# Two ScalarE copies in place of four, and two kinds of TensorE work dealt out in turn in a fused deformable convolution

## What is computed

```python
x = x + _L0_conv_ref(_gn(x), ...)
x = x + _L1_conv_ref(_gn(x), ...)

# inside _L1_conv_ref:
value = (xf @ vp_w.T + vp_b).reshape(n, L, G, cg)
om_in = depthwise_conv3x3(x, dw_w) + dw_b
om = om_in @ om_w.T + om_b            # 2*9 offsets and 9 masks for each of 8 groups
sampled = gather(y0i, x0i, (1 - ty) * (1 - tx)) + gather(y0i, x0i + 1, (1 - ty) * tx) \
        + gather(y0i + 1, x0i, ty * (1 - tx)) + gather(y0i + 1, x0i + 1, ty * tx)
out = jnp.einsum('nhwgk,nhwgkc->nhwgc', mask, sampled)
out = out.reshape(n, L, c) @ op_w.T
```

## Time and profile before

| | |
|---|---|
| median of 3 runs | 2926.51 us (2925.91 to 2933.81) |
| the profiled execution's own time | 2924.83 us |
| its span, first to last instruction | 2923.0 us |
| instructions | 100581 |
| PE (TensorE matmul) | 2430.8 us busy (83%), 40456 records |
| PEld (TensorE weight load) | 2021.2 us (69%), 40456 records |
| DVE | 2205.6 us (75%) |
| ACT (ScalarE) | 2259.7 us (77%) |
| POOL | 1917.6 us (66%) |
| mean granted TensorE clock | 0.952 of full speed |

### The profile page before, as it was taken

One profiled execution on the slowest core, in us unless ns is written; L12 is line 12 of the kernel. 1 busy time (PEld: TensorE's weight loads), 2 busy tenths in 40 slices (PEclk: granted clock), 3 DMA queues, 4 the chain that ended last, 5 costly groups with the idle time before them and its releaser, 6 DMA issues. The chain is left out here.

```text
span 2923.0 us, 100581 instructions
## 1 busy us (share of the span) xinstructions
PE 2430.8 (83%) x40456; PEld 2021.2 (69%) x40456; DVE 2205.6 (75%) x3095; ACT 2259.7 (77%) x4721; POOL 1917.6 (66%) x1452
## 2 busy tenths in 40 slices
PE   3999779993688888888888888888888888888887
PEld 2666556772577777777777777777777777777786
DVE  3555423334989897989888898989898988989773
ACT  2444256662989889898989898898989898989892
POOL 1000000003888888888988888888988898988892
PEclk8999889996899999999999999999999999999998
DMA  4555579975577677777777777777778777877675
GB/s 103 130 132 144 143 182 265 263 199 172 124 191 203 181 195 192 188 191 190 204 194 192 187 200 195 197 183 193 199 189 198 188 196 187 206 179 190 177 176 147
DMA packets 356164, 538.18 MB, mean 184 GB/s; under 512 B 171728, under 2 KB 258256, under 8 KB 355536
## 3 DMA queue, kind: packets, MB, share of 16 engines
q1 hardware_dynamic: 296656, 422.71, 60.3%
q10 hardware_dynamic: 59136, 110.11, 10.8%
HBM read 312.82 MB, written 219.77 MB: 182 GB/s over the span
## 5 line engine op out<-in xcount | busy, mean ns | idle before, releaser
L1109 ACT ACTIVATE dwt<-xp,wts 128x224 f32<-128x224 f32 x2016 | 797.3, 484 | 40.8 <-ACT wst L1135 31.8
L1280 PE MATMUL acc_p<-abuf,vbd 128*32 128x136 f32 (+5 forms) x20480 | 710.4, 291 | 54.9 <-issue 46.0
L1280 PEld LDWEIGHTS acc_p<-abuf,vbd 128*32 128x32 f32 (+1 forms) x20480 | 645.9, 145 | 117.7 <-issue 60.5
L979 DVE TENSOR_TENSOR pr<-mh_p,ht 128x864 f32<-128x864 f32 x672 | 668.9, 1051 | 23.2
L1258 PE MATMUL win_p<-pr,smat 128*128 128x160 f32 x4032 | 626.7, 310 | 27.3 <-POOL pr L1065 15.8
L246 PE MATMUL cv<-cin,wb 128*64 128x392 bf16 x6912 | 590.4, 333 | 25.8 <-ACT cin L225 25.8
L1258 PEld LDWEIGHTS win_p<-pr,smat 128*128 128x128 f32 x4032 | 570.4, 194 | 51.2 <-issue 22.4
L246 PEld LDWEIGHTS cv<-cin,wb 128*64 128x64 bf16 x6912 | 401.4, 110 | 208.7 <-ACT cin L225 25.9
L1048 POOL TENSOR_TENSOR dwt<-dwt 128x896 f32<-128x896 f32 x224 | 516.3, 2305 | 4.7 <-ACT dwt L1109 4.7
L1062 POOL TENSOR_TENSOR pr<-pr 128x576 f32<-128x576 f32 x224 | 317.3, 1417 | 187.8 <-DVE pr L979 187.8
L1135 ACT ACTIVATE wst<-win_p 128x200 f32<-128x200 f32 x896 | 388.6, 605 | 62.4 <-PE win_p L1258 38.7
(11 more groups left out here) (132 smaller groups left out, 2674.9 us busy)
## 6 DMA issues: line engine op xcount, KB each, us to landing
abuf<-weight_scratch SPq DMA_DIRECT2D x1568, 96.0 KB, 3.3
weight_scratch<-wst ACTq DMA_DIRECT2D x112, 960.0 KB, 6.2
xt<-x SPq DMA_DIRECT2D x128, 392.0 KB, 7.6
rows_scratch<-vsb SPq DMA_DIRECT2D x224, 128.0 KB, 2.1
vbd<-rows_scratch SPq DMA_DIRECT2D x896, 32.0 KB, 3.2
x_scratch<-xt SPq DMA_DIRECT2D x64, 392.0 KB, 6.6
y<-x SPq DMA_DIRECT2D x64, 392.0 KB, 4.4
x3h<-x_scratch SPq DMA_DIRECT2D x64, 392.0 KB, 4.9
```

The lines of the kernel that those rows point to most:

```text
L979: dve.tensor_tensor(pr[:, j % 2, slots, :, :, :].rearrange("p k e x z -> p e k (x z)"), mh[:, a, :, :].rearrange("p (k x) z -> p k (x z)", ...
L1109: ins = act.activation(dwt[:, j % 2, k, :].rearrange("p (r w) -> p r w", w=W), image[:, r:r + BR, k % 3:k % 3 + W], ACT.Identity, scale=dw ...
L1280: mm = pe.matmul(acc_p[32 * (2 * s + b):32 * (2 * s + b) + 32, 0:2 * TN].rearrange("p (t w r) -> p t w r", t=BR, r=2)[:, t0:t1 + 1, x0:x1, :],
```

## The change

There are four parts, which belong together.

- The order in the last 32 places of the table of offsets and masks becomes (g, k): group, then image row. `copy_om` reads its PSUM source with k innermost, that is with 256 elements between neighbours.
- `win_p` is packed: the five distances follow one another, 800 columns without gaps. The fourth distance (e == 3) then lies across the end of a 512-column bank, so its matmuls are cut into one of 32 and one of 128 columns.
- `copy_weights` takes the 800 columns in two copies of 400 elements, by the parity of the image row, in place of four of 200.
- `apply` and `windows` are dealt out in turn in three parts: four rows of `apply`, then the distances 0 and 1; four rows, distance 2; the other rows, distances 3 and 4. The waits of both stand in the first part, the semaphores that they raise in the last.

```diff
@@ -59,7 +59,6 @@
 CT = 5
 RT = 5
 RP = RT + 1
-WP = 172
 PC = 2 * BR * RP * 2
 BAND = CT * PC
 PX = 4
@@ -958,9 +957,9 @@
                 def copy_om(i, j):
                     dve.wait_ge(om_ready, NT * i + j + 1)
                     dve.tensor_tensor(
-                        oms[:, j % 2, :, :].rearrange("q w (b k g) -> q (w b) k g", b=2, g=GS),
-                        om_p[:, :].rearrange("q (k z) -> q k z", k=BR)[:, :, 0:OMC].rearrange("q k (v g) -> q v k g", g=GS),
-                        ombt[:, :].rearrange("q (v g) -> q v g", g=GS).unsqueeze(2).broadcast_to([LANES, 6 * TAPS, BR, GS]),
+                        oms[:, j % 2, :, :].rearrange("q w (g k) -> q (w g) k", k=BR),
+                        om_p[:, :].rearrange("q (k z) -> q z k", k=BR)[:, 0:OMC, :],
+                        ombt[:, :].unsqueeze(2).broadcast_to([LANES, OMC, BR]),
                         ALU.add).then_inc(om_ok, 1)
 
                 def mask_hats(i, j):
@@ -1129,13 +1128,12 @@
                     if u == 0:
                         wait(act, w_out, 16 * (t // 2))
                     act.wait_ge(win_ok, t + 1)
-                    for k in range(BR):
-                        to = 2 * BR * (2 - 2 * (k % 2)) + BR * u + k
+                    for r in range(2):
+                        to = 4 * BR * (1 - r) + BR * u + r
                         cells = wst[:, 0, to:to + 1]
                         ins = act.activation(
-                            bass.AP(cells.tensor, cells.offset, [cells.ap[0], [PC, CT], [2 * BR, 2 * RT], [BAND, GS]]),
-                            win_p[:, 0:CT * WP].rearrange("p (e z) -> p e z", e=CT)[:, :, 0:RT * BR * G].rearrange(
-                                "p e (m k g) -> p e m k g", k=BR, g=GS)[:, :, :, k, :],
+                            bass.AP(cells.tensor, cells.offset, [cells.ap[0], [PC, GS * CT], [2 * BR, 2 * RT], [2, 2]]),
+                            win_p[:, 0:CT * RT * BR * G].rearrange("p (m g k r) -> p r g m k", g=GS, k=2, r=2)[:, r],
                             ACT.Copy)
                     ins.then_inc(wst_ok, 1)
 
@@ -1247,30 +1245,34 @@
                             om = offset_row(i, j, k, s)
                     om.then_inc(om_ready, 1)
 
-                def windows(i, j):
+                def windows(i, j, part):
                     t = NT * i + j
-                    wait(pe, wst_ok, t)
-                    pe.wait_ge(mg_ok, t + 1)
-                    for e in range(CT):
+                    if part == 0:
+                        wait(pe, wst_ok, t)
+                        pe.wait_ge(mg_ok, t + 1)
+                    for e in ((0, 1), (2,), (3, 4))[part]:
                         terms = [(a, b) for a in range(3) for b in range(3) if 2 - (a + b - 2) == e]
-                        to = WP * e
+                        cuts = (0, 1, RT) if e == 3 else (0, RT)
                         for n, (a, b) in enumerate(terms):
-                            mm = pe.matmul(win_p[:, to:to + 160], smat[:, e, :],
-                                           pr[:, j % 2, 0:RT, a, b, :],
-                                           start=n == 0, stop=n == len(terms) - 1)
-                    mm.then_inc(win_ok, 1)
-
-                def apply(i, j, half):
+                            for m0, m1 in zip(cuts, cuts[1:]):
+                                mm = pe.matmul(win_p[:, BR * G * (RT * e + m0):BR * G * (RT * e + m1)], smat[:, e, :],
+                                               pr[:, j % 2, m0:m1, a, b, :],
+                                               start=n == 0, stop=n == len(terms) - 1)
+                    if part == 2:
+                        mm.then_inc(win_ok, 1)
+
+                def apply(i, j, half, part):
 
                     D, y0 = (NT * i + j) // 2, BR * j
-                    pe.wait_ge(a_in[half], 16 * READS[half] * (D + 1))
-                    if half == 0:
+                    if part == 0:
+                        pe.wait_ge(a_in[half], 16 * READS[half] * (D + 1))
+                    if half == 0 and part == 0:
                         for b in range(j + 1 if j else 0, min(j + 3, NT)):
                             pe.wait_ge(vb_in[b % VSLOT], 4 * 16 * (2 * i + b // VSLOT + 1))
                         wait(pe, accs_ok, D)
                     qb, K, x0, x1 = ((0, 128, 0, 34), (1, 96, 30, W))[half]
                     rows = range(max(0, y0 - 2), min(H, y0 + 2 * BR + 2))
-                    for yq in rows:
+                    for yq in rows[4 * part:4 * part + 4]:
                         t0, t1 = max(0, yq - y0 - 2) // 2, min(2 * BR - 1, yq - y0 + 2) // 2
                         for s in range(S):
                             for b in range(2):
@@ -1282,13 +1284,15 @@
                                     vbd[0:K, 1 - s, qb, yq // BR % VSLOT, :, :, 2 * (yq % BR) + b].rearrange("p g c -> p (g c)"),
                                     mov, start=yq == rows[0] and qb == 0, stop=yq == rows[-1] and qb == 1,
                                     skip_group_check=True)
-                    mm.then_inc(amat_ok, 1)
+                    if part == 2:
+                        mm.then_inc(amat_ok, 1)
 
                 def step(i, j, first, last):
                     n = near(i, j, -5 if j % 2 else -4, first, last)
-                    if n:
-                        apply(*n, j % 2)
-                    windows(i, j)
+                    for part in range(3):
+                        if n:
+                            apply(*n, j % 2, part)
+                        windows(i, j, part)
                     offsets_and_misc(phase(i, j), i + 1 if j == GROUPS_AT and not last else None,
                                      near(i, j, 2, first, last), near(i, j, -LAG, first, last), near(i, j, 3, first, last))
 
@@ -1302,7 +1306,8 @@
                         step(i, j, i == 0, i == pairs - 1)
                 for j in range(LAG):
                     if j < 4:
-                        apply(pairs - 1, NT - 4 + j // 2 * 2, j % 2)
+                        for part in range(3):
+                            apply(pairs - 1, NT - 4 + j // 2 * 2, j % 2, part)
                     offsets_and_misc(N + j + 3, output=(pairs - 1, NT + j - LAG))
 
         flag_far(nc, far, flag, misc)
```

## The result

The changed kernel takes 2934.3 us (median of 20 runs, 2929.9 to 3056.2; of the kernel before 2929.5 in 20 runs beside them). The ratio of the undisturbed runs is 1.0021, 95% interval 1.0014 to 1.0029: slower by a little, less than the 0.3% named as the bound of a difference, but on the other side of zero from the forecast of 2922, which was 4 us under the kernel before. The profiled execution took 2931.2 us, its span 2929.3, 6.3 more than before.

A forecast was written before the change was run, and what follows sets the result against it. DVE and POOL were taken to bound the kernel in turn, with TensorE close behind. +7 us for the earlier wait and -11 for stalls made -4 against the median 2926.5: 2922 us, own range 2914 to 2930, overall 2908 to 2956.

The forecast's parts named there:

- What bounds the kernel: DVE sets the pace in steps 0 to 3 and 5 to 8, POOL in 9 to 13; TensorE is close.
- ScalarE's copies: Two copies out of PSUM instead of four: 0.5 us a step gained, shortening nothing itself, paying for the copies starting later.
- rival in which copy_om slows: DVE's PSUM read with 256 elements between neighbours takes longer; at double time +108, about 3030 us; chance 0.08.
- The cut: Contraction matmuls at e == 3 on TensorE: eight records instead of four, +0.33 us a step, bounds 0 and 1.0.
- The passages: TensorE's switches between 128x32 tiles and the full array: two more each way from dealing out, +0.6 us a step.
- room of 0.85: TensorE's slack in us a step in the POOL-paced steps: two TensorE steps take 15.41 against POOL's 17.12.
- Stalls: TensorE's waits on instructions inside apply cost 15 us; three quarters won back, -11 us, bounds 0 and -15.
- The earlier wait: Windows' waits after apply's first part make TensorE 0.3 to 0.6 us late by step 13: +7 us in all.
- second rival: TensorE becomes the bound in steps 9 to 13, from an added 0.85 us a step on: 2955 us; chance 0.24.
- pairs of 134.9 us: Sign that the forecast is right: a pair of images takes about 134.9 us on average.
- TensorE as the bound: In steps 9 to 13, at an added 1.3 us a step: +40 less 11, 2955 us; chance 0.24.
- The faster rival: TensorE's added work stays under its slack, nothing is late and all stalls go: -15, 2911 us; chance 0.24.

The follow-up runs named there:

- slow_copies_dealt: Kernel without the cut, dealt out in three parts, with four tiny ScalarE copies ahead of the two: -19 us against the kernel before.
- no_cut: Changed kernel with contraction rows moved 32 columns up in win_p so none is cut; two copies, layout and dealing stay: -16 us against the kernel before.
- change_busy_wait: Changed kernel with twelve extra matmuls in step 9 between the first weight sums and the wait for the merge: -9 us against the kernel before.
- no_cut_plus4: Kernel without the cut, with four more 160-column matmuls a step behind the last contraction row: +84 us against the kernel without the cut.

## Why the prediction was wrong

**What bounds the kernel, ScalarE's copies, copy_om.** Right: the loss stands in the steps that POOL paces, and none in steps 0 to 6. The copies gained more than taken (0.79 us a step for 0.5), and pay nothing of their own, as said; that they pay for the earlier wait is not borne out: slow_copies_dealt, with longer copies, is no slower than no_cut. The rival in which copy_om slows is out (1.055 us).

**The cut.** Right as a price: 0.34 us a step measured, 0.33 forecast. What it does was underrated: without it the same change is 21 us faster.

**The passages.** Mis-sized: 0.73 to 0.75 us a step for two more each way, forecast 0.6. Together with the cut TensorE's step grew by 1.04 to 1.07 (forecast 0.93): 0.20 over the room of 0.85, and not 0.08.

**Stalls.** Right in kind, too small: nearly all of them went (1.5 us left of 56.7), so the whole 15 us count as won, where 11 were taken. By the rule of the Trainium skill weighed there (Runtime: NRT & Kernel Launch, Instruction fetch mechanics), that crossing into the next block is mostly hidden, nothing would have come back; the rows above, 0.5 and 1.0 us left of 56.7, disagree. That the sum by this rule, about 2934, is the measured time is chance.

**The earlier wait: the step that failed.** The prediction put TensorE's lateness behind the earlier wait at 0.4 us a pair, +7 us in all, and the clock behind that wait at nothing. From a pair without a lost slot (134.1 us, as in no_cut) to 136.00 the runs show 1.9 us a pair, some 27 us. It has two parts, about equal.

The first is the added work. change_busy_wait, where the low clock is gone, still loses 14 slots in 14 pairs, 0.9 us a pair. That is lateness rounded up: next to free until mask_hats misses the gap between two of POOL's additions, then a whole slot at once. The prediction had no such rounding, but the size of the loss doesn't come from it: the measured excess of 0.20 us a step, counted as the prediction counts its second rival, gives 0.20 x 88 = 18 us in all. So the size comes from the excess, which was taken as 0.08.

The second is the idle wait, which the prediction did not have at all: TensorE idles 2.75 us in step 9 and is low-clocked for 6.8 us after it in nine pairs. change_busy_wait shows this to be worth 14 us, the other 16 slots.

Less the 15 for the stalls, and less 5 because the pairs without either got shorter (134.45 to 134.1, for which no run gives the cause), 27 leaves the loss of 7. So the forecast is only 12 us off by luck: the cost was 20 us too low and the gain 9 too low, and the two misses partly cancel.

**The signs.** Of those named as right, few stalls and shorter copies (0.94 us a step) were there, pairs of 134.9 us were not. In the step of the merge at 1543.15 TensorE's value rows begin 1.15 us after POOL's last addition (1541.61 + 0.67), where 0.5 was the bound, and DVE waited 2.95 us for misc, where past 2.4 was named as wrong:

```profile
1543.43 0.27 PE L1193 MATMUL misc<-wts,xp 64*64 64x64 f32 x2
```

**The rivals.** TensorE as the bound was the nearest in mechanism (decides from 0.85 on), and no_cut_plus4 is that case in full: by its sum 83 us, 84 measured. The faster rival's 2911 us is the time of no_cut: what it needed was a step under the room.

Open: why the layout without dealing lengthens the stalls (earlier weight writes may, not shown), why the cut alone costs 11 us, and what in the layout gains 11 us with dealing.

## What to carry to other kernels

Where an engine's result must meet a gap in another engine's work, look for its lateness in whole slots: find in the trace how much later it may come (here some 0.1 us past an addition's end), and what one missed gap costs (0.87 us). For the total take the excess over the room times the steps, and measure the added work before trusting a room that it nearly fills. A wait that is moved ahead of independent work can cost twice, as here: the work queued behind it, and the clock after the idle time. Leave the one step whole in which the wait is long. Here that, with the contraction rows moved 32 columns up so that none is cut, gives 2905.3 us, faster than both kernels (ratio to the kernel before 0.9929, 0.9914 to 0.9945).

## What the hardware showed unasked

Twelve useless matmuls in an idle wait of 2.75 us made a kernel 14 us faster, since the granted clock stayed at 1.00. A ScalarE copy of 200 elements out of PSUM takes 350 ns in the new layout and 605 in the old one. Of the stalls without a wait, each of the 38 over 0.6 us in the kernel before ended 1.27 to 1.90 us after an instruction packet had come.
